# Key scores first, query scores half a unit later, in a fused decoder layer

## The reference

```
kv = _ln(x, kvn_w, kvn_b) @ kv_w + kv_b
q = (_ln(x, qn_w, qn_b) @ q_w + q_b).reshape(b, c, HEAD, HD).transpose(0, 2, 1, 3)
...
q = _rotary(q, x, rh_w, rh_b)
k = _rotary(k, x, rh_w, rh_b)
qn = _ln(q, ln_w, ln_b)
kn = _ln(k, ln_w, ln_b)
scores = jnp.einsum('bhqd,bhkd->bhqk', qn, kn) / np.sqrt(HD).astype(np.float32)
attn = jax.nn.softmax(scores, axis=-1)
a = jnp.einsum('bhqk,bhkd->bhqd', attn, v)
...
return a @ out_w + out_b
```

## Time and profile before

| | us |
| --- | --- |
| median of 3 executions | 2420.73 (2419.41 to 2424.11) |
| profiled execution, its time | 2423.02 |
| profiled execution, its span | 2421.0 |
| TensorE busy | 1945.1 (80%) |
| VectorE busy | 1546.8 (64%) |
| ScalarE busy | 908.2 (38%) |
| GpSimd busy | 951.5 (39%) |
| mean granted clock of TensorE | 0.901 of full speed |

### The profile page before, as it was taken

One profiled execution on the slowest core, in us unless ns is written; L12 is line 12 of the kernel. 1 busy time (PEld: TensorE's weight loads), 2 busy tenths in 40 slices (PEclk: granted clock), 3 DMA queues, 4 the chain that ended last, 5 costly groups with the idle time before them and its releaser, 6 DMA issues. The chain is left out here.

```text
span 2421.0 us, 30214 instructions
## 1 busy us (share of the span) xinstructions
PE 1945.1 (80%) x9560; PEld 1426.2 (59%) x9560; DVE 1546.8 (64%) x2943; ACT 908.2 (38%) x1532; POOL 951.5 (39%) x849
## 2 busy tenths in 40 slices
PE   4587887878888798788975799999948887788772
PEld 4455565555656465565633688888837665666651
DVE  4567667576675666767562666667654776767765
ACT  2143433334333343334341322222214555555653
POOL 1666756467564674746620222222201212221221
PEclk9688998989989898999987899999979999989985
DMA  3123132131311212222122211211031121022111
GB/s 128 26 53 87 37 94 48 48 85 36 95 47 50 77 36 74 69 57 70 38 77 101 78 53 60 79 69 53 18 107 37 52 70 49 22 69 70 53 35 52
DMA packets 90746, 148.67 MB, mean 61 GB/s; under 512 B 16560, under 2 KB 19632, under 8 KB 90672
## 3 DMA queue, kind: packets, MB, share of 16 engines
q1 hardware_dynamic: 90672, 147.76, 20.5%
HBM read 63.82 MB, written 33.55 MB: 40 GB/s over the span
## 5 line engine op out<-in xcount | busy, mean ns | idle before, releaser
L467 DVE TENSOR_REDUCE a_neg_max<-a_max 128x1 f32<-128x512 f32 x512 | 344.5, 687 | 267.3 <-PE a_max L726 258.8
L632 ACT ACTIVATE a_probs<-a_exp 128x512 f32<-128x512 f32 x512 | 290.7, 595 | 571.1 <-PE a_exp L741 568.5
L726 PE MATMUL a_max<-a_stack 96*128 96x512 f32 x512 | 235.9, 476 | 150.7 <-DMA a_stack<-a_nT_lo 100.6
L726 PEld LDWEIGHTS a_max<-a_stack 96*128 96x128 f32 x512 | 103.2, 206 | 245.4 <-DMA a_stack<-a_nT_lo 106.8
L1497 POOL TENSOR_TENSOR f_mixed<-f_tw,f_beta 128x512 f32<-128x512 f32 x64 | 96.1, 1522 | 352.2 <-DVE f_beta L1596 177.0
L311 POOL TENSOR_TENSOR a_rstd<-a_rstd,a_minus_half 128x16 f32<-128x16 f32 x64 | 186.5, 2914 | 85.0 <-DVE a_rstd L452 85.0
L703 PE MATMUL a_t<-a_w_hi,a_zT_hi 128*128 128x384 f32 x512 | 196.5, 384 | 13.4 <-DVE a_v L433 11.5
L741 PE MATMUL a_exp<-a_stack 100*128 100x512 f32 x512 | 193.5, 419 | 6.5 <-ACT a_probs L632 4.5
L704 PE MATMUL a_t<-a_w_lo,a_zT_hi 128*128 128x384 f32 x512 | 194.8, 380 | 0.0
L705 PE MATMUL a_t<-a_w_hi,a_zT_lo 128*128 128x384 f32 x512 | 193.0, 377 | 0.0
L305 POOL TENSOR_TENSOR a_n<-a_n,a_mean 128x512 f32<-128x512 f32 x64 | 67.2, 1050 | 309.8 <-DVE a_mean L441 309.6
(11 more groups left out here) (240 smaller groups left out, 4865.7 us busy)
## 6 DMA issues: line engine op xcount, KB each, us to landing
a_stack<-a_nT_hi SPq DMA_DIRECT2D x512, 64.0 KB, 2.0
a_stack<-a_nT_lo SPq DMA_DIRECT2D x256, 64.0 KB, 2.0
a_z<-x SPq DMA_DIRECT2D x8, 1024.0 KB, 7.4
a_y<-x SPq DMA_DIRECT2D x8, 1024.0 KB, 5.5
x<-a_y SPq DMA_DIRECT2D x8, 1024.0 KB, 4.4
r_xn<-x SPq DMA_DIRECT2D x8, 1024.0 KB, 5.6
r_cn<-ctx SPq DMA_DIRECT2D x8, 1024.0 KB, 7.7
x<-r_xn SPq DMA_DIRECT2D x8, 1024.0 KB, 4.3
```

The source lines that it names most:

```text
L467: nc.vector.tensor_reduce(neg_max[:, t, ROW + h:ROW + h + 1], bank_max[i % 2][:, :], AX_X, ALU.max, negate=True).then_inc(max_done, 1)
L632: nc.scalar.activation(probs[:, kt % 2, h, :], bank_exp[i % 2][:, :], ACT.Exp, scale=float(1.0 / np.sqrt(np.float32(HD)))).then_inc(exp_do ...
L726: mm(bank_max[i % 2][:, :], stack[0:ROW, par, h, t * P:(t + 1) * P], stack[0:ROW, par, HG + h, :], start=True, stop=True).then_inc(score_d ...
```

## The change

Only the tables that place the work in the steps change, with two small consequences in the code. The SP part is not touched, nor is what each piece of work computes.

- Key scores of U: from steps 1 to 12 to steps 0 to 9. Query scores of U + 1: from steps 0 to 13 to steps 5 to 14, eight in every five steps.
- The last item of the projection still stands in step 9 (before: step 8). `weigh`: from steps 5, 8, 11, 14 to 4, 6, 9, 11.
- `transpose_max` and `save_max`: from step 14 to 15; `save_max` now stands ahead of `x_norm` and `z_high` of its step.
- `turn_heads`: from steps 9, 11 to 10, 12; `turn_low` stays in 11, 13. The fourth `save_qkv`: from step 9 to 10.
- `normalise`: from step 15, 15 and the next unit's 0, 1 to steps 12, 13, 15 and the next unit's 0. `attn_hi` and `attn_low`: from steps 2 and 3 to step 1.
- `x_stats` (g = 2): from steps 6, 8, 10, 12 to 0, 1, 2, 3. `x_final` (g = 3): from 6 to 3.
- g = 0: the first output item from step 10 to 11, `add_out` of it from 11 to 12.

```diff
-QS_DONE = tuple(T * HG * min(i + 1, 14) // 14 for i in range(16))
-KS_DONE = tuple(T * HG * min(i, 12) // 12 for i in range(16))
...
+KS_DONE = tuple(8 * min(i + 1, 10) // 5 for i in range(16))
+QS_DONE = tuple(8 * max(min(i - 4, 10), 0) // 5 for i in range(16))
...
-X_NORM_AT, STATS_AFTER, FINAL_AFTER, SHIFT_AFTER = (5, 6, 7, 8), (6, 8, 10, 12), 6, 12
+X_NORM_AT, STATS_AFTER, FINAL_AFTER, SHIFT_AFTER = (10, 10, 11, 11), (0, 1, 2, 3), 3, 12
...
-NORM_AFTER, ATTN_HIGH_AT, ATTN_LOW_AFTER = (15, 15, 0, 1), 2, 3
+NORM_AFTER, ATTN_HIGH_AT, ATTN_LOW_AFTER = (12, 13, 15, 0), 1, 1
...
-            for c in range(2, T):
-                normalise(G * B - 1, c)
+            normalise(G * B - 1, T - 1)
...
+                    if i == SAVE_MAX_AT and left >= 1:
+                        save_max(U + 1, (g + 1) % 2)
                     for t in range(T):
                         if g == 0 and left == 4 and i == X_NORM_AT[t]:
                             x_norm(b + 1, t)
                         if g == 0 and left == 4 and i == Z_HIGH_AT[t]:
                             z_high(b + 1, t)
-                    if i == SAVE_MAX_AT and left >= 1:
-                        save_max(U + 1, (g + 1) % 2)
```

More of the change, by code:

```diff
@@ L28 @@
 DVE_STEPS, POOL_STEPS = 55, 40
-QS_DONE = tuple(T * HG * min(i + 1, 14) // 14 for i in range(16))
-KS_DONE = tuple(T * HG * min(i, 12) // 12 for i in range(16))
[L33 to L36, removed]
+KS_DONE = tuple(8 * min(i + 1, 10) // 5 for i in range(16))
+QS_DONE = tuple(8 * max(min(i - 4, 10), 0) // 5 for i in range(16))
+PROJECT_DONE = (3, 5, 7, 8, 9, 11, 12, 13, 15, 16, 16, 16, 16, 16, 16, 16)
+WEIGH_AT = (4, 6, 9, 11)
+TURN_AT, SAVE_AFTER = (10, 12), (2, 4, 7, 10)
+OUT_AT, ADD_AFTER, OUT_BANK = (11, 12, 15, 15), (12, 13, 15, 15), (1, 1, 0, 1)
 Z_AT, Z_HIGH_AT, Z_LOW_AFTER = (13, 13, 14, 14), (13, 13, 15, 15), (13, 14, 15, 15)
-MAX_AT, SAVE_MAX_AT = 14, 14
-X_NORM_AT, STATS_AFTER, FINAL_AFTER, SHIFT_AFTER = (5, 6, 7, 8), (6, 8, 10, 12), 6, 12
+MAX_AT, SAVE_MAX_AT = 15, 15
+X_NORM_AT, STATS_AFTER, FINAL_AFTER, SHIFT_AFTER = (10, 10, 11, 11), (0, 1, 2, 3), 3, 12
 MEAN_AFTER, VAR_AFTER, SQUARE_AT = (0, 1), (3, 4), (1, 2)
 TURN_HIGH_AT, TURN_LOW_AFTER = (10, 12), (11, 13)
-NORM_AFTER, ATTN_HIGH_AT, ATTN_LOW_AFTER = (15, 15, 0, 1), 2, 3
+NORM_AFTER, ATTN_HIGH_AT, ATTN_LOW_AFTER = (12, 13, 15, 0), 1, 1
 SIDES = (1, 0)
```

## The result

| | before | after |
| --- | --- | --- |
| median | 2422.42 us (4 runs) | 2689.58 us (4 runs, 2687.23 to 2691.39) |
| ratio | 1 | 1.110, 95% interval 1.1077 to 1.1123 |
| span of the profiled execution | 2421.0 us | 2689.4 us |
| TensorE busy | 1945.1 us | 2042.9 us |
| VectorE busy | 1546.8 us | 1546.2 us |

Slower by 267 us, where 77 were forecast. TensorE is busy 98 us longer with the same products; VectorE is busy as long as before.

A forecast was written before the change was run, and what follows sets the result against it. TensorE was taken to set the pace, its idleness counting. Units of +7.0, -5.4, +13.4 and +0.9 us gave +15.9 a full batch, +80 for five; with batches 0, 6 and 7, +77 on 2421.0: 2498 us, range 2440 to 2550.

The forecast's parts named there:

- The start of a unit: Steps 0 to 4: key scores, exponentials and attention chain ahead of the first save add 1.0 us a unit.
- The lower clock: TensorE's slower level behind idleness: 1.7 us at a unit's start, 2.2 us behind z's hole in g=2.
- The end of a unit: VectorE's list of maxima and normalisations outlasts TensorE's work: 5.0 us of new idleness, the unit ending at 29.9 us.
- the wait for z: In g=2 VectorE waits for z, landing 20.6 us in; TensorE loses 19.7 us plus 2.2 us of lower clock.
- The wait for regrouping: Query scores at unit starts no longer wait for regrouping transfers: 12.9 us a batch removed, 6.5 us once at the first unit.
- z does not bind: Rival: in g=2 z lands before step 0 ends or what waits has slack; 2380 us, faster; chance 0.05.
- the start is dearer: Rival: chain before the first save costs 1.5 us more in 29 units, 44 us; 2542 us; chance 0.15.
- the end is cheaper: Rival: normalisations slip into holes, half of the 5.0 us goes, 52 us less; 2446 us; chance 0.10.
- g=0: Unit with output projections and turns of z: 51.9 us, before 44.88, so +7.0 us.
- Batch 0: No output projection to be late and the 6.5 us wait lost: +7 us.
- Batch 6: Loads no x, so has no z wait: -4 us.
- Batch 7: Little projection, key and query scores wait less for each other's engines: about -6 us, a guess between -12 and +6.

The follow-up runs named there:

- e5_early_z: `e2_short` with z's load issued in unit g=1, ahead of that unit's regrouping transfers: 2571.11 us.
- e2_short: The changed kernel with eight copies ahead of the attention phase merged into two, leaving VectorE 168 instructions ahead of the loop: 2653.78 us.
- e6_attn: `e4_both` with `attn_hi` and `attn_low` back in steps 2 and 3: 2537.83 us.
- e11_norm_z: `e10_norm_fit` with z's load issued ahead of the regrouping of unit g=1: 2453.18 us.
- e12_before_z: The kernel before with only z's load issued ahead of the regrouping of unit g=1: 2390.84 us.
- e9_shift_z: The kernel before with query scores in steps 3 to 13 and z's load issued ahead of the regrouping of unit g=1: 2335.66 us.
- e1_stats: The changed kernel with the statistics of z back in steps 6, 8, 10, 12 of unit g=2: 2625.87 us.
- e4_both: The changed kernel with the edits of both `e1_stats` and `e2_short`: 2583.79 us.
- e10_norm_fit: The changed kernel with z's statistics, normalisations and attention parts at the places of before, copies unmerged, 172 instructions ahead of the loop: 2499.01 us.
- e3_before_long: The kernel before with each of eight copies ahead of the loop cut in two halves, 180 instructions ahead of the loop: 2444.21 us.

## Why the prediction went wrong, point by point

Three steps of the sum failed. The start of a unit was priced at 1.0 us on top of the work, and in the unit followed below it took 5.0; undoing the early attention parts alone gave 46 us. The lower clock was given 2.2 us more a batch, and it took some 7. And VectorE's stop behind the loop's jump back, 36 us, had no term at all. The end of a unit was a little too cheap, the wait for z too dear.

**The wait for regrouping goes: right.** No row of a_max waiting for a_stack is left, 12.9 us a batch.

**z in g=2: right in mechanism and in time, too dear in size.** VectorE's wait was forecast at about 17 us, six times; it was 107.1 us in six, 17.85 each. z came 20.1 us into the unit (forecast 20.6), the held-up projection 25.5 us (25.3). The row in this batch, with the mean ahead of it at 779.55, and TensorE's behind it:

```profile
797.31 0.69 DVE L382 BATCH_NORM_STATS2 a_stats<-a_z 128x6 f32<-128x512 f32 x1 [17.59 <-DMA a_z<-x]
```

```profile
802.73 0.69 PE L702 MATMUL a_t<-a_w_hi,a_zT_hi 128*128 128x384 f32 x1 [17.36 <-DVE a_v L433]
```

19.7 + 2.2 us was the price in the sum. It measured 13.8 us a batch when z came early (`e5_early_z` against `e2_short`), and g=2 of batch 6, which loads no z, is 37.2 against 54.1: 16.9. That the stall hides other waits of the unit, which cost time again once it is gone, is only argued. The rival "z does not bind" is excluded.

By the fit in the Trainium skill ("DMA: Bandwidth & Descriptors", Anatomy of one DMA), which is stated for the path over POOL, z would by estimate have come 3 us sooner. These loads are issued by SP, and the trace does not bear that time out for them: z landed 7.5 us after its issue (median of eight).

**The start of a unit: failed, in size.** "It comes to about 8.5 us ... I count 1.0 us a unit." g=3 of the profiled batch reached the end of its third weighing 26.6 us after its start, where the steps of the forecast give 22.6. The windows from its start to the item of step 4, from there to that end, and on to the next unit:

```profile
831.30:840.39 9.09, 8.00 (x33) 7.09 (x31) 4.52 (x12) 5.04 (x7) 3.65 (x4) 0.77 0.43 101
840.39:857.88 17.49, 16.67 (x91) 8.89 (x91) 9.06 (x26) 7.25 (x13) 11.81 (x8) 0.90 0.10 23
857.88:869.42 11.54, 6.87 (x40) 3.46 (x37) 10.13 (x18) 1.19 (x2) 9.23 (x13) 0.86 0.10 22
```

The chain to the first save, through `attn_low` and the mean, was seen and nearly rightly counted: the item of step 4 started 9.1 us into the unit, 8.3 (7.3 and 1.0) in the forecast. What had no term stands behind it: 17.5 us where 14.3 were counted, of which TensorE is idle 0.8 us (842.00, waiting for exponentials) and for the rest longer busy, at the lower clock at first (843.21). The rival "the start is dearer" had 1.5 us for 29 units, 44 us; `e6_attn` gives 46 us for the attention parts alone.

**The end of a unit: right in mechanism, too cheap.** The waits stand where they were said to, ahead of the last scores and the transposes:

```profile
864.88 1.09 PE L725 MATMUL a_max<-a_stack 96*128 96x512 f32 x2 [1.65 <-DVE a_neg_max L467]
...
868.68 1.09 PE L731 MATMUL a_max<-a_ident,a_neg_max 128*100 128x128 f32 x4 [2.71 <-DVE a_neg_max L467]
```

From the end of the third weighing (857.88) to the next unit's first product (869.42) it took 11.5 us against 10.0 forecast: 4.7 us idle, where the forecast has 5.0, and 6.9 us busy, where it has 5.0. Putting the normalisations back gave 39 us. The rival "the end is cheaper" is excluded.

**g=0: two waits right, the unit too short.** The two waits counted one by one came out as counted: the turn of z behind `turn_low` 1.83 us (1.9), the output projection 3.31 us (3.3):

```profile
717.97 1.25 PE L695 MATMUL a_t<-a_ident,a_z 128*128 128x128 f32 x8 [1.83 <-DVE a_nT_lo L458]
...
728.67 0.79 PE L759 MATMUL a_t<-a_wo_hi,a_attnT_hi 128*128 128x512 f32 x1 [3.31 <-DVE a_zT_lo L422]
```

Yet the unit took 58.0 us and not 51.9, and the first of these waits ended 39.7 us into it and not 35.2 (32.5 and 2.7 for the start). TensorE is busy 47.47 us in it at a clock of 0.82, before 40.62 us at 0.96, with 222 and 220 products: 6.9 us more, where the forecast added 1.7 for the clock.

**The clock as a term: failed, in size.** The forecast has 7.3 us of lower clock a batch (3.4 in g=0, 2.2 in g=2, 1.7 in g=3) in place of 5.1: 2.2 us more. TensorE's busy time grew by 12.4 us a batch. Not all of this is the clock. The trace's records of the granted clock, laid over TensorE's busy time, put 22.3 us of the batch before at the lower level and 38.6 us of this one; with 0.32 us for a projection product in place of 0.18, that is some 7 us more, an estimate.

The clock does not account for the rest. From the first to the last save of the maxima, `before` and `e11_norm_z` have as many products and the same mean clock, and yet 42.6 us lie between their busy times (of which 177.0 and 175.4 us are at the lower level):

```profile
115.98:1267.26 1151.28, 969.48 (x5188) 649.12 (x5186) 758.64 (x1502) 445.42 (x736) 688.52 (x640) 0.91 0.24 62
115.70:1300.03 1184.33, 1012.06 (x5188) 636.33 (x5186) 764.27 (x1503) 450.33 (x736) 687.64 (x640) 0.91 0.23 60
```

A likely part of it is waiting that no idle time shows. Two query scores that maxima release 0.6 us apart stand as one busy stretch (row 864.88), since a row lasts longer than the 0.24 us that a score costs. How much that is was not measured. Nor is the difference between `e11_norm_z` and `e12_before_z` mainly the clock: 175.4 and 136.6 us at the lower level make some 17 us of their 62, an estimate in the same way.

As to the clock, the forecast had its lower level only behind a unit's start and z's hole (and once in g=0). The rows show it a second time in g=3 (843.21), behind idleness of 0.40, 0.70 and 0.82 us. How the chip decides is settled by no run here. The rows show the four units of after, with 6.6 to 22.3 us of idleness, at 0.75 to 0.88, and three of `e9_shift_z`, with 3.0 to 4.0 us, at 1.00.

**The hole behind the loop's branch: not in the forecast.** 36 us by `e2_short`. The Trainium skill ("Runtime: NRT & Kernel Launch", Instruction fetch mechanics) states that a taken branch whose target is no longer held by the engine forces a fetch by DMA before it can go on. The trace agrees in kind, with 5.8 us and the packets on queue 14; I had not weighed that rule. The change adds two instructions to VectorE ahead of the loop, four with waits, and the listing of instructions shows that, but not what it does. Holes came with 166, 174 and 180 instructions ahead of the body, none with 168 and 172. Each comparison moved the body by six or eight instructions; two alone were never tried, and what separates 166 from 168 was not settled.

**The sum.** Batches 1 to 5: 38.8 us each more than before (955.8 against 761.7) where +15.9 was forecast, 115 us missing. Batch 0: +35.5 against +7. Batch 6, -4 forecast: it was +22.7 (167.1 against 144.4), the order of work without z and, but for g=0, without the loop. Batch 7, -6 forecast: +15.5. Together 191 us. By edit, each kernel against the one ahead of it in this chain, from 2689.6 on: `e1_stats` -64 (place of z's statistics), `e4_both` -42 (hole), `e6_attn` -46 (attention parts), `e10_norm_fit` -39 (normalisations), `e11_norm_z` -46 (z's early load): 2453, still 27 us above the kernel before. What the lower clock took is in each of these and no item of its own.

The chance of 0.92 for slower was borne out; the range up to 2550 was not. Each rival moved one term and left the others at the forecast's value, but the terms of a unit share one clock and one ordered list, and all but z's were too small together. One sum among the rivals is rounded too far: 12.9 and 5 us in eight batches make 143 us, hence 2278 and not 2285; nothing rests on it.

## What to carry to other kernels

When work is moved to the head of a stage, write down for each engine what stands behind the first instruction that will wait, follow it to the end of the stage, and price that too, not only the length of the waiting chain. Count small idleness of TensorE at more than its length: compare the busy time of the same products in a quiet and in a broken stage of the trace before, and put the difference into the sum. Compare the packets of the instruction queue and the waits with the cause issue before looking for a reason in the order of work. The gain that this change sought lay in one of its halves (query scores late) together with an issue that it did not touch (z's load ahead of the regrouping): 2336 us, 3.7% under the kernel before.

## What the runs showed of the hardware

- VectorE's loop can stand still for 5 to 6 us at each jump back (five times 5.2 us in `e3_before_long`, 5.8 us in the changed kernel), with the cause "issue", and whether it does hangs on six or eight instructions ahead of the loop: 22 us for the kernel before, 28 to 42 us for the variants of the kernel after. The count of instruction packets in the table of queues tells it at once: 37 or 38 without, 62 or 63 with.
- 158 products kept TensorE busy for 27.1 us at a granted clock of 1.00 (`e9_shift_z`), 29.5 at 0.88 and 31.8 at 0.75 (the changed kernel). But busy time also grew at the same clock, 969.5 to 1012.1 us for 5188 products at 0.91: it is not a measure of the clock alone.
- Removing 50 us of waits of VectorE for z took 72 us off the kernel with late query scores; TensorE was busy 32 us less.
